# Summing the exponentials of attention: VectorE's part of each slot handed to GpSimd

## What is computed

```python
x = x + attention(layernorm(x), ...)      # first layer; the change is in here
x = x + moe_ffn(layernorm(x), ...)
x = x + gated_attention_unit(layernorm(x), ...)
x = x + gated_ffn(x, ...)

# attention, for each batch b, group g, head h of the group:
dots = einsum('bghqd,bgkd->bghqk', qg, k) * scale
attn = softmax(dots, axis=-1)
out  = einsum('bghqk,bgkd->bghqd', attn, v)   # then @ Wout
```

## Time and profile before

| | us |
|---|---|
| median of three executions | 996.5 |
| lowest, highest | 996.47, 1002.62 |
| the profiled execution, its own time | 1002.83 |
| its span, first to last instruction | 1001.0 |
| VectorE busy | 725.2 |
| GpSimd busy | 596.7 |
| matmuls of TensorE busy | 856.8 |

### The profile page before, as it was taken

One profiled execution on the slowest core, in us unless ns is written; L12 is line 12 of the kernel. 1 busy time (PEld: TensorE's weight loads), 2 busy tenths in 40 slices (PEclk: granted clock), 3 DMA queues, 4 the chain that ended last, 5 costly groups with the idle time before them and its releaser, 6 DMA issues. The chain is left out here.

```text
span 1001.0 us, 13168 instructions
## 1 busy us (share of the span) xinstructions
PE 856.8 (86%) x4752; PEld 441.8 (44%) x4752; DVE 725.2 (72%) x1042; ACT 467.3 (47%) x811; POOL 596.7 (60%) x325
## 2 busy tenths in 40 slices
PE   2975899999999999798389999999999964999688
PEld 1533444444444444344144444444444422575346
DVE  5796787887788788458678788788778756246763
ACT  1762355445554555368145554555554532435221
POOL 0573467767776777539247776776777753055500
PEclk9996799999999999899699999999999975999889
DMA  5000000000000000000000000000000002000001
GB/s 150 0 1 1 0 2 1 2 1 1 2 1 1 2 1 1 1 1 1 1 1 1 2 1 1 2 2 1 1 1 1 2 3 64 22 1 0 1 1 43
DMA packets 49451, 7.96 MB, mean 8 GB/s; under 512 B 42470, under 2 KB 47978, under 8 KB 49386
## 3 DMA queue, kind: packets, MB, share of 16 engines
q1 hardware_dynamic: 47610, 6.07, 4.0%
q10 hardware_dynamic: 1776, 1.05, 0.4%
HBM read 5.92 MB, written 1.05 MB: 7 GB/s over the span
## 5 line engine op out<-in xcount | busy, mean ns | idle before, releaser
L346 POOL TENSOR_TENSOR space<-space 128x1024 f32<-128x1024 f32 x160 | 389.1, 2432 | 68.0 <-ACT space L591 50.1
L723 DVE TENSOR_REDUCE part<-psum 128x2 f32<-128x1024 f32 x256 | 312.5, 1221 | 120.2 <-PE psum L431 120.2
L591 ACT ACTIVATE space<-psum 128x512 f32<-128x512 f32 x512 | 264.7, 602 | 205.4 <-PE psum L451 205.4
L463 PE MATMUL psum<-space,vb 128*64 128x512 f32 x1024 | 247.5, 605 | 0.0
L431 PE MATMUL psum<-kh,qh 64*128 64x512 f32 x512 | 133.5, 518 | 65.7 <-DVE part L723 60.0
L351 POOL TENSOR_TENSOR space<-space 128x1024 f32<-128x1024 f32 x30 | 71.6, 2385 | 134.2 <-DVE space L737 134.2
L431 PEld LDWEIGHTS psum<-kh,qh 64*128 64x128 f32 x512 | 49.9, 191 | 204.0 <-DVE part L723 168.2
L463 PEld LDWEIGHTS psum<-space,vb 128*64 128x64 f32 x1024 | 62.3, 136 | 106.4 <-issue 100.5
L451 PE MATMUL psum<-qh,kh 64*128 64x512 f32 x512 | 103.4, 400 | 0.0
L451 PE MATMUL psum<-qh,kl 64*128 64x512 f32 x512 | 102.3, 395 | 0.0
L451 PE MATMUL psum<-ql,kh 64*128 64x512 f32 x512 | 102.3, 395 | 0.0
(11 more groups left out here) (160 smaller groups left out, 998.1 us busy)
## 6 DMA issues: line engine op xcount, KB each, us to landing
ql<-nmx SPq DMA_DIRECT2D x256, 0.5 KB, 2.0
x<-in_L_attn_x SPq DMA_DIRECT2D x2, 512.0 KB, 7.0
w1s<-in_L_ffn_W SPq DMA_DIRECT2D x4, 256.0 KB, 2.8
w2s<-in_L_ffn_W SPq DMA_DIRECT2D x4, 256.0 KB
out<-x SPq DMA_DIRECT2D x4, 256.0 KB, 2.0
wproj<-in_L_attn_Wq SPq DMA_DIRECT2D x1, 512.0 KB, 5.3
wout<-in_L_attn_Wout SPq DMA_DIRECT2D x1, 512.0 KB, 10.2
wproj<-in_L_attn_Wkv SPq DMA_DIRECT2D x2, 128.0 KB, 5.5
```

The costliest lines, as they stand in the source:

```text
L346: pool.tensor_tensor(to, pt[0] if u == 1 else to, pt[u], ALU.add)\
L463: last = pe.matmul(outp[rows(h), :], vb[:, place(m)[1], kt, :], pt[kt][:, h, :], start=(kt == 0), stop=(kt == TILES - 1))
L591: act.activation(pt[kt][:, h, :], key_scores[kt % 2][h], ACT.Exp).then_inc(exp_made, 1)
L723: dve.tensor_reduce(to[:, half, :], scores.rearrange("p (h k) -> p h k", h=2), AX_X, ALU.max, negate=True)\
```

## The change

GpSimd adds all seven tiles of a slot to the first (seven adds, L346), in every slot but the last of each batch. VectorE's `add_tail` and GpSimd's add of `tail` are gone in those slots. In the last slot of each batch everything is as before: five adds by GpSimd, `tail` by VectorE, and both are given to TensorE as terms of the sum. The counts on the semaphores follow: `pool_added` rises by 7 a slot, `tail_made` by 2 a batch. ScalarE's exponentials of tiles 6 and 7, which had waited for `tail_made` of the slot before, now wait for GpSimd's add of that tile.

```diff
-ADDED = 5
-ADDS = ADDED + 1
+ADDS = 7
+LATE = 5
...
                     to = acc[n % 2]
-                    for u in range(1, ADDED + 1):
+                    for u in range(1, TILES if m < SLOTS - 1 else LATE + 1):
                         pool.wait_ge(exp_made, 2 * (TILES * n + u + 1))
...
                         pool.tensor_tensor(to, pt[0] if u == 1 else to, pt[u], ALU.add)\
-                            .then_inc(pool_added, 1 if m < SLOTS - 1 or u < ADDED else 2)
-                    if m < SLOTS - 1:
-                        pool.wait_ge(pool_added, ADDS * n + ADDED)
-                        pool.wait_ge(tail_made, 2 * (n + 1))
-                        pool.tensor_tensor(to, to, tail, ALU.add).then_inc(pool_added, 1)
+                            .then_inc(pool_added, 1 if m < SLOTS - 1 or u < LATE else ADDS + 1 - LATE)
...
                     if m == SLOTS - 1:
-                        pe.wait_ge(tail_made, 2 * (n + 1))
+                        pe.wait_ge(tail_made, 2 * (b + 1))
...
                         act.wait_ge(pv_made, TILES * (n - 1) + kt + 1)
-                        if kt <= ADDED:
-                            act.wait_ge(pool_added, ADDS * (n - 1) + max(kt, 1))
-                        else:
-                            act.wait_ge(tail_made, 2 * n)
+                        act.wait_ge(pool_added, ADDS * (n - 1) + max(kt, 1))
...
                     dve.wait_ge(exp_made, 2 * TILES * (n + 1))
-                    if m:
-                        dve.wait_ge(pool_added, ADDS * n)
                     dve.tensor_tensor(tail[:, h, :], pt[TILES - 2][:, h, :], pt[TILES - 1][:, h, :], ALU.add).then_inc(tail_made, 1)
...
-                    if k == 3 and -1 <= m < SLOTS - 1:
-                        add_tail(m + 1, 0)
+                    if k == 3 and m == SLOTS - 2:
+                        add_tail(SLOTS - 1, 0)
...
-                    if k == 3 and -1 <= m < SLOTS - 1:
-                        add_tail(m + 1, 1)
+                    if k == 3 and m == SLOTS - 2:
+                        add_tail(SLOTS - 1, 1)
```

## The result

The changed kernel takes 1011.66 us (median of four, 1009.09 to 1012.28) against 997.11 for the kernel before (its three executions and a fourth): ratio 1.0129, 95% interval 1.0088 to 1.0169. It is slower by 1.3%; the prediction said 1010.3. The profiled execution took 1009.09, with a span of 1007.3. The granted clock of TensorE was 0.944 to 0.947 in these executions, and 0.937 to 0.945 in those of the kernel before that ran beside the experiments, so the clock doesn't explain that the changed kernel is slower.

What follows compares the result with a forecast made beforehand. TensorE's work plus about 1 us a slot of late VectorE reductions was taken as the bound. 25 slots x 0.59 = 14.8, less 1.0 for two batch ends, gave +13.8 on 996.5: 1010.3 us, range 995 to 1023.

Steps and rivals of the forecast that it cites:

- What delays TensorE: Each slot: about 1 us of late VectorE reductions, set by which two-SBUF-input VectorE operation stands behind a GpSimd add.
- three coincidences in one slot: GpSimd adds end at 215.65, 218.18, 220.96; VectorE's L729, L747, L729 end at 215.67, 218.74, 220.98.
- The walk: One slot followed from 206.35 with seven adds following their exponentials: +0.60 in k1, +0.59 in k2, still +0.59 at k0.
- "not slower" rival: GpSimd's adds pace themselves and lag, so their ends stay where they stand now: 995.5 us; 18% with similar cases.
- add 1 of the next slot: GpSimd's first add after add 7: ends at about 226.8, then GpSimd idles before add 2 at 229.0.
- The sum: 25 slots x 0.59 = 14.8 us, less 0.5 at each batch's end: +13.8 on 996.5, 1010.3.
- The race after add 6: In k3, add 7 beats L754 to the port by a 0.07 us margin: 2.45 a slot, +64, 1074 us; 8%.
- Costed at nothing: Removing VectorE's tail adds in k3 saves nothing, being covered by TensorE's second unit; uncovered, 0.68 a slot.
- L729's wait in k1: L729 stands behind add 4, ends at 216.27 instead of 215.67, and delays k2's second unit by 0.60.

Runs made afterwards that it cites:

- the order experiment: Kernel before, with GpSimd's first add of a slot put ahead of its add of the last slot's tail: 1023.7 us, ratio 1.026.
- the extra wait: Changed kernel, with GpSimd's fourth add of a slot also waiting for the maximum of k1: 987.0 us, ratio 0.989.
- the kernel with the tails back: Changed kernel, with VectorE's add_tail made again in every slot, its result unused but in the last slot: 1029.3 us, ratio 1.031.
- The later kernel that was to set the two against each other: Kernel before, with each maximum by one tensor_reduce and GpSimd's fourth add held until the maximum directly ahead of the scaling: 975.4 us.

## Why the prediction was right

- *What delays TensorE.* That a VectorE operation with two SBUF inputs waits for the running add to end was read from three coincidences in one slot. It held in every kernel. In the twelve traces 282 corrections begin during an add of GpSimd, and all end 0.54 to 0.56 us after its end; so do 676 of 677 two-input minima, 0.01 to 0.03 after it (the last began just as the add ended). The 445 minima made by tensor_reduce during an add take 0.16 each, and the 1887 reductions of PSUM 1.21 to 1.23. Both the order experiment and the extra wait show that this, and not GpSimd's load by itself, sets the slot. The Trainium skill ("SBUF — State Buffer", Who interferes with whom) says that a VectorE instruction with at most one input in SBUF, outside its two-port modes, doesn't contend with GpSimd; the tensor_reduce at 0.16 us in the middle of adds agrees.
- *The walk.* Forecast and measured: add 4 starts 2.48 after the unit of k1, 2.47; the minimum of k1 ends 4.87 after it, 4.86; second unit of k2 2.49 after the first, 2.46; a slot of 20.18, 20.17. Add 6 was to end 2.22 after the correction, and ends 2.24 after it (220.67 less 218.43). The chain of adds followed the exponentials and did not pace itself: add 4 had idled 0.16 for tile 4's, and adds that meet nothing take 2.34 to 2.40. That is why the "not slower" rival failed.
- *A step of the walk that was wrong*: add 1 of the next slot. I put it at 226.8, behind the start of k0. It starts directly behind add 7, at 223.46 where k0 starts at 225.65, some 2.5 us earlier than forecast. So the minimum of k3 stands behind it and takes 1.57 instead of 0.16, which I had not foreseen, and which is over half of the 70 us more that L722 is busy. It costs no time only because VectorE has nothing due after it until k0; in the kernel with the tails back this same add delays the second tail add and TensorE. The next add 2 waits for its exponential in any case, so the rest of the walk stands.
- *The sum.* Forecast +14.8 for the slots and -0.5 for each end, 13.8 in all. Measured in the profiled executions: +13.8 for the slots, -1.5 and -0.7 for the ends, 11.6 in all. The 1.0 less in the slots lies in the first ones of each batch, which I counted at the steady price. The medians differ by 14.5, so some 3 us of that lie outside what the two profiles show in the attention. Single executions of the kernel before lie 6 us apart (996.47 to 1002.62). So the price of a slot is confirmed (0.58 for 0.59); that the total came within 1.4 us of the median is in part luck.
- *The race after add 6* went to VectorE in every slot but the last two of a batch: L745 takes 0.68, and add 7 is shown 0.20 to 0.21 us behind it. The later kernel that was to set the two against each other has the add 0.22 behind (250.79 against 250.57), no closer, and the same winner. How narrow the margin is, no run shows. A scaling that waits for a whole add was seen only at the batches' ends, in the kernel before too (2.76 us, at 395.10 and 407.05). In the changed kernel one is at 412.98 (2.75). There an add shown from 412.54 had been waiting since before the end of the correction (412.94); it ends 2.24 after that end, and the scaling 0.55 after the add.
- *Costed at nothing*, the tails: right against the kernel before, and the cover is thinner than I said. I named TensorE's second unit as the cover; the runs show that it also takes an idle GpSimd (otherwise 0.54 a slot). Had the change kept the tails beside the seven adds, that would have been an error of some 25 x 0.54 = 13 us.
- *The step that was put wrongly*: L729's wait in k1 as what costs 0.60. Without that wait the slot is shorter by 0.08 and not by 0.6, because the correction waits for add 5 in any case. The sum was right because the second wait gives the same end.

## What to carry to other kernels

When operations of one engine wait for another's to end, look at where the other's long operations end, not at how busy the engines are: of two kernels with the same arithmetic one was 2.6% slower, and one wait more took the changed one from 1.3% above the kernel before to 1.1% below it. A very short operation with a long mean duration in the groups is the sign to look for, but count its wait only after asking what the operation behind it waits for. Moving work between such engines also takes away what held a queue in place: with the add of the tail gone, GpSimd's chain moved earlier, and the end of another add, 0.6 us later, came to lie over the minimum of k1. And follow every operation of the walk to its own release: the one that I didn't, add 1, moved by 2.5 us, and that it cost nothing was luck.

## What I had not expected

That one input less changes an operation so wholly: a tensor_reduce of 128x4 takes 0.16 us in the middle of adds under which the tensor_tensor of 128x2 takes 0.56 to 2.02 in the steady slots. And that busy time moved against the work: 60 operations less on VectorE, and 34 us more of busy time.
